# Two attention layers in one kernel: the next image's first value unit one slot later, and two DMA transposes of slot 15 in the other order

## The reference, cut to what matters

```
t, p = W_theta x + b, W_phi x + b          # 64 channels
x1 = x + W_fuse (x softmax(t' p / 8)') + b  # layer 0: 1024 x 1024 scores
h = group_norm(x1)                          # 32 groups
q, k, v = W_q h + b, W_k h + b, W_v h + b
y = x1 + W_p (v softmax(q' k / sqrt(128))') + b   # layer 1
```

## Time and profile before

| | |
|---|---|
| median of 3 runs | 1777.76 us (1776.36 to 1781.32) |
| profiled execution | 1780.63 us |
| its span, first to last instruction | 1778.8 us |
| busy: TensorE, VectorE, ScalarE, GpSimd | 95%, 80%, 79%, 81% |
| DMA queue of SyncE, share of 16 engines | 81.4% |
| granted TensorE clock, mean | 0.992 of full speed |

### The profile page before, as it was taken

The page is one execution under the profiler, slowest core; times in us unless marked ns, Lnnn a source line. Parts: engine busy times, 40 slices in busy tenths (PEclk is TensorE's granted clock), DMA queues, the critical chain, the costliest instruction groups (busy, mean ns, idle before and its releaser), DMA issues.

```text
span 1778.8 us, 34679 instructions
## 1 busy us (share of the span) xinstructions
PE 1686.0 (95%) x8970; PEld 1112.1 (63%) x8970; DVE 1414.7 (80%) x1605; ACT 1399.3 (79%) x2088; POOL 1442.2 (81%) x1513
## 2 busy tenths in 40 slices
PE   4799999999999999999999999999999999999986
PEld 3466666666666666666666666666666666666653
DVE  5588878888888888888888888788888888888864
ACT  3488878778888778888888888788888887888864
POOL 3589878888888889888889888889888888888863
PEclk9799999999999999999999999999999999999999
DMA  2589888788888888888888888888888888878874
GB/s 63 105 150 168 166 164 174 161 167 171 163 175 168 169 163 173 168 175 162 172 162 165 176 169 169 166 160 167 178 167 170 174 160 167 175 160 176 161 143 101
DMA packets 860086, 286.33 MB, mean 161 GB/s; under 512 B 822304, under 2 KB 823200, under 8 KB 860064
## 3 DMA queue, kind: packets, MB, share of 16 engines
q1 hardware_dynamic: 860064, 286.08, 81.4%
HBM read 50.86 MB, written 17.04 MB: 38 GB/s over the span
## 4 chain that ended last, share of the span: by engine, by line
PE 66%; issue 13%; DVE 8%; ACT 7%; POOL 2%; DMA 1%; ACTq 0%; SPq 0%; DVEq 0%; POOLq 0%
PE o_ps L447 26%; PE s_ps L447 22%; PE m_ps L447 11%; PE s_ps L487 7%; DVE neg_max L753 3%; DVE pair L770 2%; ACT e L652 2%; ACT s_ps L652 2%; ACT h_hi L631 1%; DVE stats L817 1%; ACT et L662 1%; DMA et<-pair 1%; DVE den_scaled L782 1%; DVE x L807 0%; DVE theta L841 0%
## 5 line engine op out<-in xcount | busy, mean ns | idle before, releaser
L447 PE MATMUL o_ps<-et,v_hi 128*128 128x512 f16 x2048 | 696.6, 382 | 28.3 <-issue 18.2
L753 DVE TENSOR_REDUCE neg_max<-s_ps 128x1 f32<-128x1024 f32 x512 | 624.7, 1220 | 98.2 <-PE s_ps L447 96.4
L447 PE MATMUL o_ps<-et,v_lo 128*128 128x512 f16 x1024 | 389.8, 381 | 0.0
L447 PEld LDWEIGHTS o_ps<-et,v_hi 128*128 128x128 f16 x2048 | 202.9, 99 | 269.8 <-issue 78.4
L447 PE MATMUL s_ps<-phi,theta 128*128 128x512 f32 x1024 | 332.1, 447 | 12.5 <-ACT e_copied L652 4.8
L770 DVE SCALAR_TENSOR_TENSOR pair<-s_ps,pair 128x1024 f16<-128x1024 f32 x256 | 311.9, 1218 | 38.5 <-ACT pair L677 38.1
L652 ACT ACTIVATE s_ps<-s_ps,neg_max 128x1024 f32<-128x1024 f32 x256 | 278.1, 1086 | 53.1 <-DVE neg_max L753 49.6
L907 POOL TENSOR_TENSOR pair<-e_copied,pair 128x1024 f16<-128x1024 f32 x128 | 274.1, 2141 | 22.2 <-ACT pair L675 22.2
L764 DVE SCALAR_TENSOR_TENSOR et<-s_ps,et 128x1024 f16<-128x1024 f32 x128 | 156.8, 1225 | 153.9 <-ACT et L662 153.9
L677 ACT ACTIVATE pair<-s_ps 128x1024 f16<-128x1024 f32 x256 | 261.9, 1023 | 17.6
L447 PE MATMUL s_ps<-k_hi,q_hi 128*128 128x512 f32 x512 | 248.9, 486 | 5.0 <-POOL q_lo L907 2.1
(11 more groups left out here) (132 smaller groups left out, 2937.3 us busy)
## 6 DMA issues: line engine op xcount, KB each, us to landing
rden_row<-rden_dram SPq DMA_DIRECT2D x128, 256.0 KB, 3.9
xs<-in_x SPq DMA_DIRECT2D x32, 512.0 KB, 4.7
phi<-phi SPq DMA_DIRECT2D x64, 256.0 KB, 3.1
out_y<-y_sb SPq DMA_DIRECT2D x64, 256.0 KB, 3.4
et<-pair SPq DMA_TRANSPOSE x384, 4.5
rden_dram<-rden SPq DMA_DIRECT2D x128, 2.0 KB, 2.2
w_f<-in_w_fuse_t SPq DMA_DIRECT2D x1, 64.0 KB, 2.7
ident_sb<-in_ident SPq DMA_DIRECT2D x1, 64.0 KB, 2.3
```

Source lines behind the costliest of these rows:

```text
L447: mm = pe.matmul(out, lhs_t, rhs, start=start and n == 0, stop=stop and n == len(terms) - 1)
L753: nc.vector.tensor_reduce(neg_max[:, t % 4:t % 4 + 1], s_ps[:, part(t), :], AX.X, ALU.max, negate=True).then_inc(s_max, 1)
```

## The change

Two numbers of tables change. `v0` stands in slot 15 instead of 14, and the transpose of the copied tile 12 is issued in slot 15 instead of 14. The second has an effect on the order of the queue, since in slot 15 `transposes` first deals with the crossed tile 13 and then with the copied one. `LO_SLOTS` stays: GpSimd still writes tile 12's low half in slot 14.

```diff
-COPIED_OUT_SLOTS = {0: 3, 4: 8, 8: 11, 12: 14}
+COPIED_OUT_SLOTS = {0: 3, 4: 8, 8: 11, 12: 15}
...
 UNITS = {0: "gn1", 1: "gn2", 2: "v1", 4: "k0", 5: "k1", 6: "q0", 7: "w0", 8: "q1", 9: "mx", 10: "tp0", 11: "w1",
-         12: "tp1", 14: "v0"}
+         12: "tp1", 15: "v0"}
```

## The result

| | before | after |
|---|---|---|
| median of 6 runs each | 1776.99 us | 1767.57 us (1765.46 to 1769.14) |
| profiled execution's span | 1778.8 us | 1766.0 us |
| 28 images of the loop, each | 53.11 us | 52.58 us |

The ratio is 0.9941, with a 95% interval from 0.993 to 0.9953: 10.5 us faster by the ratio, 9.4 by the medians, where 7.5 were forecast. The two profiled executions lie 12.8 us apart in their spans; a profile is of one execution, and that of the kernel before took 1780.63 us, 3.6 more than the median here.

The account below looks back on a forecast made before the run. TensorE, busy 1686.0 of 1778.8 us, was taken as the bound, only its idle time winnable. 4.5 + 6.5 - 3.5 = 7.5 us off the median 1777.76 gave 1770.3 us, range 1765.4 to 1779.

Parts of the forecast that it names:

- Term A: Slot 2, tiles 12 to 15: first transpose issued 0.85 us earlier shrinks TensorE's landing waits from 5.6 to 1.1, gaining 4.5 us.
- The dry DMA engines: Slot 15: the DMA engines' share is 0.00 from 870.90 to 872.20, so they are free for the earlier transpose.
- the variant of a first issue that is held longer: Tile 13's issue held 0.85 us longer by a draining broadcast, nothing won at slot 2: 1777; chance 0.33 with the absorbed case.
- Term B: Slot 6, tiles 0 to 3: tile 1's transpose issue ends 0.5 us sooner; landing waits fall from 8.8 to 2.3, gaining 6.5 us.
- the two reads behind it the same 0.5 us: SyncE queue: next image's load and the reciprocals' broadcast read start about 0.5 us earlier, like the store ahead of them.
- Term C: Give-back: TensorE arrives earlier at unmoved waits for `e`, losing about 0.2 us in each of roughly 18 images, -3.5 us.
- The moved unit: v0's matmuls behind tile 15's scores: no work added, zero effect on TensorE, ScalarE and GpSimd.
- The rival of a late copy of v0: ScalarE copies v0 too late, delaying tile 15's exponential: at worst 21 us, less the 7.5, giving 1792; chance 0.07.
- The sum: Whole program: the gains at slots 2 and 6 less the give-back, 4.5 + 6.5 - 3.5 = 7.5 us less.
- Absorbed: Slot 6 gain doesn't come or more is given back: 3 us remain, 1774.8; chance 0.33 with the variant of 1777.

Follow-up runs that it names:

- experiment 9: The changed kernel run once more, unedited, beside the kernel before on another chip: ratio 0.993.
- experiment 3: Changed kernel, with SyncE waiting for tile 12's low half before tile 13's transpose, order kept: 1786.24 us, ratio 1.003 to the kernel before.
- experiment 4: Kernel before, with the load of the next image issued in slot 4 instead of slot 1: 1786.35 us, ratio 1.003.
- experiments 6 to 8: VectorE's row sums' product split: in two on the changed kernel (0.9987) and the kernel before (1.002), in four single columns on the changed kernel (0.9981).
- Experiment 2: Kernel before, with only v0 moved from slot 14 to 15, the copied tile's transpose staying in slot 14: 1782.36 us, ratio 1.0007.

## Why the prediction was right

The direction and mechanism held: the two landing waits, the earlier start, and nothing from v0. The sizes of the terms did not, and that their errors partly cancelled is luck. By its own steps:

- *Term A, slot 2, 4.5 us.* The first issue came at -3.53, exactly 0.85 us earlier, and tile 14's landing 0.8 to 0.9 us earlier. The seven listed waits of 5.6 us became one of 0.18, so 5.4 us were recovered. Three were forecast to keep 1.1 together, each behind a landing that took 5.6 to 5.7 us; in this execution the two longest took 5.2 and 5.3 us, and one of them made the 0.18. That is chance: in the changed kernel's second profile (experiment 9) the longest took 5.5 and 5.7 us, and three waits of 1.5 us stayed. The cause, the time of the first issue, is shown by experiment 3.
- *The dry DMA engines.* The row of 0.00 began at 870.90, but the new issue was to come at 870.22, where the share was still 0.47 in the trace before (870.20 to 870.90). After the change the engines in fact finish what they had 0.6 us after the first issue (median of the 28 images). It did no harm, since that issue's own packets start 1.2 us behind it in both kernels; so the variant of a first issue that is held longer didn't come (1.92 us before, 1.94 after, medians).
- *Term B, slot 6, 6.5 us.* The waits of 8.8 us became 0.9 in two images, 7.9 recovered. The step that was too small is "the two reads behind it the same 0.5 us". The store of the reciprocals did start 0.5 us earlier (4.38 against 4.88), but it then held the queue 0.48 us instead of 0.79, and the reads came 0.8 us earlier. Tile 1's issue shrank by 1.1 us in the median here, but by 0.6 us in the second profile of the same kernel. That the place of the reads matters for the transposes behind them is shown by experiment 4, where all waits at slot 6 went with the load.
- *Term C, -3.5 us.* The listed waits for `e` grew by 4.9 us. That they move with VectorE's chain is shown by experiments 6 to 8, where 0.1 us more of its time per group raised them to 23.3 and 30.0 us. Beside them new waits for VectorE's `x` came, which the forecast didn't have.
- *The moved unit, zero.* ScalarE was forecast to have 0.55 us to spare and has 0.55. Experiment 2 gives 1.0007. The rival of a late copy of v0 is refuted.
- *The sum, 7.5 us.* By listed waits the loop's gain would be about 6 to 7 us, yet the 28 images lost 15.0 us: 9.5 of idle time and 5.5 of *busy* time, though TensorE did the same work. The profile hides part of every wait. A matmul's end is modelled, and where nothing is waited for the next one starts about 0.16 us before it, so a wait is listed shorter by that; and idle times up to 0.15 us aren't listed at all. The first value product of a group at slot 2, with the matmul ahead of it, in an image of the kernel before that lists no wait there:

```profile
669.44 0.28 PE L447 MATMUL m_ps<-w_f_hl,x_hi 128*128 128x128 f32 x1
669.67 0.39 PE L447 MATMUL o_ps<-et,v_hi 128*128 128x512 f16 x1
```

It starts 0.23 us after the matmul ahead; after the change this is 0.11 to 0.12 us in an undisturbed image (610.00 and 610.11 there), so this one waited 0.11 us and no row says so. The two images of experiments 6 to 8 show the same: the second is 0.34 us longer by one wait, of which the row lists 0.19 as idle, and the stretches book 0.18 more as busy:

```profile
1437.31 0.38 PE L447 MATMUL o_ps<-et,v_hi 128*128 128x512 f16 x1 [0.19 <-DVE x L807]
```

```profile
1338.83:1391.23 52.40, 51.66 (x280) 34.44 (x280) 43.98 (x50) 43.59 (x68) 45.07 (x47) 1.00 0.83 170
1391.23:1443.97 52.74, 51.84 (x280) 34.46 (x280) 44.34 (x50) 43.62 (x68) 45.05 (x47) 1.00 0.83 169
```

Taken from the starts of the matmuls, with the hidden part of each wait, the 28 images of the loop give this (us):

| waits of TensorE | before | after | change | forecast |
|---|---|---|---|---|
| landings, slot 2 | 10.8 | 0.5 | -10.3 | -4.5 |
| landings, slot 6 | 13.3 | 2.2 | -11.1 | -6.5 |
| for `e` | 23.5 | 28.7 | +5.2 | +3.5 |
| for VectorE's `x` | 0.0 | 3.6 | +3.6 | none |
| all else | | | -2.4 | |
| the 28 images | 1487.1 | 1472.1 | -15.0 | -7.5 (whole program) |

The terms that were mis-sized are therefore A and B: the forecast counted 14.4 us of landing waits where there were 24.1, as 4 us were hidden in the 25 listed ones and the rest in waits too short to be listed. What came back was mis-sized as well, 8.8 us instead of 3.5. The one error covers half of the other. Of "all else" 0.6 us are landings at slot 10, and 1.8 us I can't assign. The loop's 15.0 us is also more than the 9.4 to 10.5 of the result: the spans of the two executions lie 12.8 apart, and the one before was slower than its median.

- *"Absorbed"* (0.33) was wrong in that term B came in full, right in that four tenths of the recovered waits (8.8 of 21.4 us) came back as waits for `e` and `x`.

## What to carry to other kernels

A queue that waits for the inputs of one transfer keeps every later transfer back: where two are due at nearly the same time, issue first the one whose inputs are ready first, and look whether the DMA engines are idle meanwhile; 0.85 us of earlier start in each image was worth 10 us here. When an engine waits just before a consumer of DMA data and the named releaser was long done, compare the landing time with the start. A wait's row can be too short by the overlap of the modelled matmul ahead of it, and short waits have no row, so compare the starts of matmuls and the lengths of whole repeats, too. Before a range is built on the waits of one execution, look at a second one.

## What the runs showed of the hardware that I had not expected

- A VectorE operation of 128x4 elements took 0.21 us or up to 1.30 us, depending on whether a GpSimd operation was running; the long ones all end within 83 ns of its end. Single columns are never held (512 of 512 at 201 to 209 ns, 306 of them wholly inside a GpSimd operation).
- How long the issue of a DMA transpose holds SyncE changed with what stood ahead of it: about 2 us with little ahead, 3.29 in the median behind a load of 512 KB and a broadcast of 256 KB, 2.14 with these 0.8 us earlier (2.65 in another execution of the same kernel), and 2.78 with the load moved away.
- The first packets of a transpose begin 1.2 us after its issue (1.23 in the median image, in both kernels); in the earlier trace rows the engines are idle until 872.20 with the issue at 871.07.
- 0.13 us more delay of one issue per image went with 5.7 us more of listed waits at slot 2 (one execution of each).
